# The stores of the other heads of batch 0 wait for the second half of the first loads, and maximum units from the eleventh on get one filler matmul in place of two

## The reference

```python
mod = (silu(c) @ wmod).reshape(2, 6, 1, -1)
sa, ca, ga, sb, cb, gb = (mod[:, i] for i in range(6))      # ga, gb kept away from zero
h = layernorm(x) * (1 + ca) + sa
Q = ((h @ W_dq) @ W_uq).reshape(2, 1024, 16, 8)
K = ((h @ W_dkv) @ W_uk).reshape(2, 1024, 16, 8)
V = ((h @ W_dkv) @ W_uv).reshape(2, 1024, 16, 8)
scores = where(causal, einsum('bqhd,bkhd->bhqk', Q, K) / sqrt(8), -inf)
out = einsum('bhqk,bkhd->bqhd', softmax(scores), V).reshape(2, 1024, 128) @ W_o
x = x + ga * out
h = layernorm(x) * (1 + cb) + sb
x = x + gb * moe(h)          # shared expert + the two best of eight for each token
```

## Time and profile before

| | |
|---|---|
| three runs | 491.86, 496.24, 515.8 us, median 496.24 us |
| the profiled execution | 494.29 us, its span 492.5 us |
| mean granted TensorE clock | 0.951 |
| TensorE busy | 416.5 us, 85% of the span |
| VectorE busy | 318.2 us, 65% |
| ScalarE busy | 267.9 us, 54% |

### The profile page before, as it was taken

The page is one execution under the profiler, slowest core; times in us unless marked ns, Lnnn a source line. Parts: engine busy times, 40 slices in busy tenths (PEclk is TensorE's granted clock), DMA queues, the critical chain, the costliest instruction groups (busy, mean ns, idle before and its releaser), DMA issues.

```text
span 492.5 us, 9009 instructions
## 1 busy us (share of the span) xinstructions
PE 416.5 (85%) x2945; PEld 244.2 (50%) x2964; DVE 318.2 (65%) x1132; ACT 267.9 (54%) x612; POOL 142.3 (29%) x235
## 2 busy tenths in 40 slices
PE   5689899899999999989999989884788987978910
PEld 3344333534435444354343442454577976867910
DVE  5677898888888879679698615468333334333607
ACT  3353657566765766666666785533254435543522
POOL 2260620000102003304210002024556566665420
PEclk9799899999999999999999998998799999999975
DMA  5334030250302003012000093000111111112043
GB/s 137 101 119 116 33 89 10 63 165 1 96 4 65 36 2 97 1 28 73 1 24 2 0 296 90 2 23 8 47 33 44 43 45 38 38 42 47 27 151 122
DMA packets 21307, 29.09 MB, mean 59 GB/s; under 512 B 3876, under 2 KB 15381, under 8 KB 20757
## 3 DMA queue, kind: packets, MB, share of 16 engines
q1 hardware_dynamic: 18333, 23.01, 15.4%
q0 software_dynamic: 2496, 5.12, 3.7%
q10 hardware_dynamic: 432, 0.39, 0.3%
HBM read 20.44 MB, written 7.80 MB: 57 GB/s over the span
## 4 chain that ended last, share of the span: by engine, by line
PE 66%; DVE 12%; issue 8%; ACT 6%; DMA 4%; another core or an unknown queue 2%; SPq 1%; POOL 0%; DVEq 0%; POOLq 0%; ACTq 0%
PE oacc L1482 14%; PE sc L1462 11%; PE mx L1433 10%; PE sc L1707 7%; PE oacc L1718 6%; PE mx L1491 2%; DVE masked L1106 2%; PE sc L1550 2%; PE sc L1467 2%; ACT osb L773 2%; DVE mxp L1110 1%; PE mx L1563 1%; DMA S<-q_parts 1%; ACT pr L877 1%
## 5 line engine op out<-in xcount | busy, mean ns | idle before, releaser
L765 ACT ACTIVATE pr<-sc 128x512 f32<-128x512 f32 (+1 forms) x304 | 157.1, 581 | 91.8 <-PE sc L1467 50.8
L1106 DVE CUSTOM_DVE_ANT_0 masked<-mx,later 128x128 f32<-128x128 f32 (+3 forms) x256 | 111.7, 486 | 14.0 <-PE mx L1433 13.3
L1433 PE MATMUL mx<-S 72*128 72x512 bf16 (+3 forms) x384 | 112.1, 329 | 9.7 <-DVE mxp L1106 2.2
L1462 PE MATMUL sc<-S 75*128 75x512 bf16 (+3 forms) x384 | 110.6, 328 | 0.6 <-ACT pr L765 0.3
L1110 DVE TENSOR_REDUCE mxp<-mx 128x1 f32<-128x512 f32 x128 | 82.6, 685 | 24.5 <-PE mx L1433 24.0
L1482 PE MATMUL oacc<-pr,vb 128*32 128x512 f32 (+3 forms) x768 | 75.2, 505 | 0.4
L877 ACT ACTIVATE pr<-sc,bcur 128x128 f32<-128x128 f32 x156 | 44.4, 373 | 45.4 <-PE sc L1707 24.5
L1462 PEld LDWEIGHTS sc<-S 75*128 75x128 bf16 x384 | 35.4, 97 | 48.4 <-issue 24.9
L1433 PEld LDWEIGHTS mx<-S 72*128 72x128 bf16 x384 | 34.2, 97 | 48.9 <-DVE mxp L1106 14.5
L1707 PE MATMUL sc<-S,vb 128*128 128x128 f32 x312 | 45.5, 293 | 9.2 <-issue 9.1
L668 POOL DMA_INDIRECT token_results<-S,goal x39 | 39.6, 1016 | 40.3 <-ACT S L892 34.5
(11 more groups left out here) (245 smaller groups left out, 465.0 us busy)
## 6 DMA issues: line engine op xcount, KB each, us to landing
S<-q_parts SPq DMA_DIRECT2D x48, 96.0 KB
S<-k_parts SPq DMA_DIRECT2D x21, 192.0 KB
S<-in_we SPq DMA_DIRECT2D x1, 2048.0 KB, 9.4
S<-in_we SPq DMA_DIRECT2D x4, 512.0 KB, 10.1
parts<-token_results SPq DMA_DIRECT2D x4, 512.0 KB, 5.5
x_sb<-in_x SPq DMA_DIRECT2D x4, 256.0 KB, 3.9
hidden_rows<-parts SPq DMA_DIRECT2D x4, 256.0 KB, 2.4
out_y<-attn SPq DMA_DIRECT2D x4, 256.0 KB, 2.3
```

The lines of the kernel that those rows point to most:

```text
L765: act.activation(pr[:, group % NBUF, h:h + n, at:at + w], src, ACT.Exp, scale=float(DK) ** -0.5).then_inc(s["exp_done"], 1)
L1106: ins = dve.tensor_tensor_reduce(masked[:, d % 2, w * m:w * m + w], mx[:, a % RING, w * m:w * m + w], later[:, HALF - w:HALF], 1.0, LOWEST ...
L1433: ins = pe.matmul(dst[:, w * m:w * m + w], S3[0:CROSS, r3, 1, q:q + P], S3[0:CROSS, r3, 0, kk:kk + w], start=(m == 0), stop=True, skip_gro ...
L1462: ins = pe.matmul(dst[:, w * m:w * m + w], S3[0:CROSS + 3, r3, 0, kk:kk + P], S3[0:CROSS + 3, r3, 1, q:q + w], start=(m == 0), stop=True, ...
```

## The change

SP waits for all six loads of `first_in1` before it issues `store_parts(0)`. Behind maximum units 10 to 19 of task 0 there is one filler in place of two (`LAST_MAX[0]` is 10).

```diff
                 load_k(0, slice(HALF * c, HALF * c + HALF), s[f"first_in{c}"])
                 sp.wait_ge(s["q_out"], 48 * c + 48)
                 load_q(0, c, s[f"first_in{c}"])
+            sp.wait_ge(s["first_in1"], 16 * 6)
             store_parts(0)
             neg_rows(0, 0)
             load(1)
@@
                 if kind == "max":
                     max_scores(t, k, a)
                     if t == 0 and k < AHEAD:
-                        fill(sc[:, 2, :], 2)
+                        fill(sc[:, 2, :], 2 if k < LAST_MAX[0] else 1)
                 elif kind == "turn":
```

## The result

The changed kernel takes 496.69 us, the kernel before 493.64 us (medians of 20 runs each). The ratio is 1.008, with a 95% interval of 1.0054 to 1.0107: slower by 2.7 to 5.3 us, about 3.9. That is inside the 2% that the forecast called no change, and clear of noise over this many runs. The quotient of the two medians is 1.006 only, because all ratios here leave out the slow runs, executions that took over 1.5% more than the fastest of the same kernel. The profiled execution took 496.13 us, its span is 494.4 us, 1.9 more than before.

A forecast was written before the change was run, and what follows sets the result against it. It took the kernel as a TensorE-bound pipeline after the start. First score unit 0.7 us later plus 0.9 us of clock gave 495.9 us on the profiled run, 497.8 on the median; forecast the middle, 496.9 us, range 491.5 to 502.

The forecast's parts named there:

- the signs that I gave: Profile after: unit 11 without wait near 36.0 us, first score unit near 45.6, span's end moving with task 1's first unit.
- Loads without the stores beside them: Before maximum unit 11: q loads usable 6.5 us after issue instead of 7.6, so unit 11 starts 1.1 us earlier.
- Rival (d): At unit 11: loads no faster without the stores, usable at 37.0 us; kernel 498.1 us; chance 0.14.
- Fillers: Units 11 to 19: one filler fewer each, 1.94 us; with the loads' gain, first score unit reached at 42.3 us.
- VectorE as the brake: Units 11 to 19: VectorE needs 0.63 us per unit against TensorE's 0.43, so first score unit 42.3 instead of 41.9 us.
- The queue behind the wait: SP queue: stores issued 35.9 to 43.3 us, `negT` 2.2 us later, first score unit at 45.6 us, 0.7 later.
- Rival (c): SP queue: stores issue in 5.8 us, `negT` early, TensorE waits 1.75 us, clock holds; 493.4 us; chance 0.18.
- Rival (f): At the added wait: it releases at once and only the fillers go; 492.8 us; chance 0.03.
- rival (e): From the first score unit: clock falls and stays down while VectorE sets the pace; 516 us; chance 0.02.
- `load(1)`: First maximum unit of task 1: issue 2.9 us later, usable about 57.8 us; counted zero, at most 0.3 us.
- The clock: Behind the first score unit: a 3.3 us standstill lowers the clock, costing 0.9 us, bounds 0 and 1.7.
- rival (b): First score unit 0.7 us later without the clock drop; the low stretch at 58.4 us may vanish; 495.0 us; chance 0.18.

The follow-up runs named there:

- fewer fillers alone: One filler fewer behind units 10 to 19, no added wait, against the kernel before: 468.51 us, ratio 0.9963; again on the other chip 470.18 us, 1.0013.
- fewer fillers, more behind scores: One filler fewer behind units 10 to 19, two fillers for one behind score units 3 to 9, no added wait, against the kernel before: 468.55 us, 0.9975.

## Why the prediction held, and where its terms were off

The forecast was 496.9 us and no change of 2%, by way of a first score unit 0.7 us later and 0.9 us of clock. The median was 496.69 us. That the numbers meet is partly luck: the forecast stood between the profiled run and the median of three, and the median of the kernel before turned out at 493.64, so the true change is about 3.9 us where I had 1.6. Of the signs that I gave, two failed in the first trace: unit 11 still waited, for 0.37 us, and the span's end moved by 1.9 us where the first maximum unit of task 1 moved by 3.16. Which executions had a low stretch elsewhere decided the latter.

- **Loads without the stores beside them.** Expected usable 6.5 us after their issue; TensorE saw them after 7.0 us (36.47 - 29.43) in the changed kernel, and SP was released after 6.9 us there and after 6.3 to 6.7 us in the five other kernels with held stores. Not held, TensorE saw them after 7.4 to 7.9 us in four kernels (fewer fillers alone, 36.51 - 29.12 and 37.00 - 29.15) and after 7.0 us in a fifth (fewer fillers, more behind scores, 36.60 - 29.57). So holding the stores gains up to 1.5 us there, about 0.8 by the middle values, where the rows said 1.1. What I drew from the ring order in the Trainium skill ("DMA: Bandwidth & Descriptors", "Queues, rings and completion order"), that holding the stores would win nothing, does not hold here. The section does not promise it either: it says too that a later descriptor may finish its write before an earlier one. Rival (d) is out.
- **Fillers.** TensorE reached the first score unit at 46.01 - 2.85 = 43.2 us, not 42.3: 0.5 us is the later start, the rest mostly the smaller gain from the fillers. With fewer fillers alone the stretch from unit 11 took 6.53 us (43.04 - 36.51) in place of 7.86, a gain of 1.3 us where I had 1.5. VectorE as the brake is shown only in part: with one filler left it is busy for 2.64 and 2.70 us of 3.00 from 37 us on, but the only wait of TensorE after unit 11 is 0.2 us for ScalarE. Waits for VectorE come with no filler at all.
- **The queue behind the wait.** Right, but for the release of SP at 36.35 us in place of 35.9: stores issued in 7.2 us (7.4 expected), `negT` usable 2.4 us after its issue (2.3), first score unit 1.1 us later (0.7). Rival (c), stores that issue in 5.8 us, is out: without loads beside them they took 7.2 us too, so it is their shape that sets it or something else that all executions share; which, was not tried. Rival (f) is out as well: SP did wait, and the stores came 4.65 us later. Of rival (e), the clock that stays down, only the beginning was seen: it came back after some 7 and 10 us.
- **`load(1)`.** I had it at most 0.3 us late and covered. In the changed kernel it was covered, but by the clock: TensorE was 2 us later anyway. With the clock up TensorE waits 0.44 to 0.48 us for it, in three kernels, and the unit comes 0.6 us late.
- **The clock.** The direction was right and the size was wrong, which is the main miss: 0.9 us expected, 2.05 in the changed kernel's trace, 3.4 in its repetition. This is the term of the sum that was mis-sized. I had taken the loss of VectorE's time in one low stretch of 3.4 us, where VectorE still had a backlog to work off. Behind a standstill there is no backlog and the low clock lasted 6 to 10 us, with VectorE busy for about half of it. The bound of 1.7 us that I gave for this term was therefore no bound.
- **What gives some of it back**: the low stretch of the kernel before at 58.4 us, which was there again in the trace of fewer fillers alone, again, and not in that of the changed kernel. I named it in rival (b) but left it out of the sum.

Open is why the low clock lasts longer in one execution than in the next. How much the mean over many executions loses to it is known only roughly: by the 2 us for each 0.01 of mean clock, the changed kernel on the later chip (0.949 against 0.959) loses about 2 of its 5 us. The profiles are single executions.

## What to carry to other kernels

Before a wait goes into a DMA queue, list what is issued behind it and when each is needed: the stores could wait, but a 12 KB transfer and the next task's operands behind them could not. A standstill of TensorE can be paid twice, once as time and once as clock. The one of 2.85 us made the first score unit 1.11 us late, as the gain ahead of it had paid for the rest, and the low clock behind it cost 2.05 us more. A filler is worth most right where the engine would stand still, and cost nothing there: with twelve of them the first score unit still waited 0.2 us for the DMA. On a stretch that TensorE itself paces fillers cost their time, 1.3 us for the first one here, down to the point at which another engine is the brake; the clock did not fall there without them. And compare a variant with the one that differs from it in the single edit: against the original, a gain from fillers hid a cost of the wait.

## What was not expected of the hardware

The same kernel before took 493.64 us in the first measurements, and 470.05, 470.08 and 469.84 us in the three sessions of the experiments, on two chips. I take the first to have been another chip. No trace of the kernel before was taken in the sessions, but up to the transposes of the expert weights the profiled executions agree to within 5 us (344.80 and 340.20 us), and from there to the end of the span it is 147.7 us in the first and 124.7 us in the second: the difference lies in the expert tiles. Groups of line, idle time and releaser there, first of the kernel before in the first measurements, then of the kernel with fewer fillers alone in a session, both from 345 us on:

```profile
L1718 PE MATMUL oacc<-vb,pr 128*128 128x128 f32 x312 | 44.2, 287 | 7.6 <-ACT pr L877 6.4 <-issue 1.2
L892 ACT ACTIVATE S<-oacc 128x128 f32<-128x128 f32 x39 | 11.3, 289 | 18.2 <-PE oacc L1718 13.6 <-remote 4.3
```

```profile
L1718 PE MATMUL oacc<-vb,pr 128*128 128x128 f32 x312 | 42.1, 278 | 0.3 <-ACT pr L877 0.3
L892 ACT ACTIVATE S<-oacc 128x128 f32<-128x128 f32 x39 | 11.2, 287 | 11.4 <-PE oacc L1718 11.1
```

In the first, ScalarE waits for 4.3 us in all for something that the profile only calls remote, and TensorE waits for ScalarE; in the second these waits are nearly gone. TensorE's idle time at line 1707, the other product of the experts, falls from 9.2 to 0.6 us too. Together these are only part of the difference, and what the waits are was not tried.
